# A transformer layer with routed experts on one core: three tiles of the last sum on TensorE, and the first and last loads in halves

## What is computed

```python
probs = softmax((gelu(xf @ wg1 + bg1) @ wg2 + bg2)[:, :20])
top_vals, top_idx = top_k(probs, 2)
gates = zeros((N, E)).at[arange(N)[:, None], top_idx].set(top_vals)
y = sum over e of gates[:, e, None] * (xf @ We[e] + be[e])
x = x + y
```

## Time and profile before

| what | us |
|---|---|
| median of three runs (674.92 to 677.53) | 677.24 |
| the profiled execution | 675.09 |
| its span, first to last instruction | 673.2 |
| last product of the last block ends | 649.05 |
| first load of `ys` issued | 653.20 |
| first scaled add begins | 658.12 |
| last scaled add ends | 669.81 |
| last store lands | 672.8 |

### The profile page before, as it was taken

The page is one execution under the profiler, slowest core; times in us unless marked ns, Lnnn a source line. Parts: engine busy times, 40 slices in busy tenths (PEclk is TensorE's granted clock), DMA queues, the critical chain, the costliest instruction groups (busy, mean ns, idle before and its releaser), DMA issues.

```text
span 673.2 us, 16124 instructions
## 1 busy us (share of the span) xinstructions
PE 642.6 (95%) x6390; PEld 526.1 (78%) x6390; DVE 439.9 (65%) x999; ACT 327.2 (49%) x620; POOL 299.4 (44%) x265
## 2 busy tenths in 40 slices
PE   5999999999999999999999999999999999999980
PEld 5778888887888788887888788887778787788850
DVE  4865666666556555757555557454477678999976
ACT  4435453544434444444433426334355654899930
POOL 2215644366344644366344614612126157788520
PEclk9999999999999999999999999999999999999995
DMA  8512566545764456445753562220000497999729
GB/s 331 210 50 47 137 168 150 128 113 137 174 137 122 121 147 148 111 125 144 174 127 77 136 168 83 80 64 2 2 18 34 146 363 272 382 389 354 285 86 339
DMA packets 41817, 105.68 MB, mean 157 GB/s; under 512 B 8052, under 2 KB 8436, under 8 KB 40962
## 3 DMA queue, kind: packets, MB, share of 16 engines
q1 hardware_dynamic: 37330, 96.12, 48.5%
q0 software_dynamic: 4400, 8.41, 3.4%
HBM read 65.61 MB, written 11.34 MB: 114 GB/s over the span
## 4 chain that ended last, share of the span: by engine, by line
PE 91%; DVE 4%; DMA 2%; ACT 1%; issue 1%; POOL 0%; POOLq 0%; DVEq 0%; SPq 0%; ACTq 0%
PE bank L195 25%; PE bank L197 23%; PE bank L196 23%; PE bank L415 5%; PE bank L397 4%; PE bank L201 3%; DVE x_sb L1854 2%; PE bank L633 1%; PE bank L620 1%; PE bank L649 1%; DMA wr<-scratch_ys 1%; DMA raw<-in_wk 1%; DMA xi<-scratch_xn,row 1%; PE bank L447 1%; DVE stats L1580 0%
## 5 line engine op out<-in xcount | busy, mean ns | idle before, releaser
L1891 POOL TENSOR_SCALAR pp<-pp,rl 128x400 f32<-128x400 f32 x128 | 164.1, 1300 | 182.4 <-DVE rl L1359 182.4
L978 ACT ACTIVATE pp<-pp,acc 128x400 f32<-128x400 f32 x128 | 79.0, 619 | 66.6 <-DVE acc L1418 66.6
L1418 DVE CUSTOM_DVE_ANT_0 pp<-bank,cap 128x400 f32<-128x400 f32 x128 | 65.9, 571 | 50.9 <-PE bank L397 50.9
L195 PE MATMUL bank<-chi,wk 128*128 128x400 f32 x248 | 87.3, 352 | 0.0
L196 PE MATMUL bank<-clo,wk 128*128 128x400 f32 x248 | 85.5, 345 | 0.0
L197 PE MATMUL bank<-chi,wk 128*128 128x400 f32 x248 | 85.5, 345 | 0.0
L1410 DVE STREAM_TRANSPOSE raw<-pp 128x512 f32<-128x512 f32 x128 | 83.4, 688 | 2.2 <-POOL pp L1891 2.2
L195 PE MATMUL bank<-wv,chi 128*128 128x512 f32 x192 | 78.8, 410 | 0.0
L196 PE MATMUL bank<-wv,chi 128*128 128x512 f32 x192 | 75.4, 393 | 0.0
L197 PE MATMUL bank<-wv,clo 128*128 128x512 f32 x192 | 75.2, 392 | 0.0
L195 PE MATMUL bank<-wh,xu 128*128 128x512 f32 x144 | 59.7, 415 | 0.4 <-ACT hT L912 0.2
(11 more groups left out here) (268 smaller groups left out, 1333.6 us busy)
## 6 DMA issues: line engine op xcount, KB each, us to landing
pt<-raw SPq DMA_DIRECT2D x256, 128.0 KB, 2.4
wr<-in_We SPq DMA_DIRECT2D x13, 1024.0 KB, 12.1
craw<-in_ctx SPq DMA_DIRECT2D x15, 800.0 KB, 4.6
raw<-in_We SPq DMA_DIRECT2D x8, 1024.0 KB, 13.2
acc<-in_We SPq DMA_DIRECT2D x6, 1024.0 KB, 12.6
wr<-scratch_ys SPq DMA_DIRECT2D x8, 512.0 KB, 8.1
x_sb<-in_x SPq DMA_DIRECT2D x2, 1024.0 KB, 11.5
scratch_xn<-acc SPq DMA_DIRECT2D x8, 256.0 KB
```

The costliest lines, as they stand in the source:

```text
L195: pe.matmul(o, lhs[0], rhs[0], start=start, stop=False)
L978: act.activation(frame(p8), frame(p8), ACT.Exp, bias=bias, scale=-1.0, accum_out=total).then_inc(S["a_exp"], 1)
L1418: dve.tensor_tensor_reduce(out=frame(p8), in0=scores[:, p8 % 4, :], in1=cap[:, :], scale=-1.0, scalar=nm[:, b, p8:p8 + 1] if seg else 3e38 ...
L1891: pool.tensor_scalar(frame(p8), frame(p8), rl[:, n % 2, p8:p8 + 1], None, ALU.mult).then_inc(S["g_pn"], 1)
```

## The change

Tiles 2, 4 and 6 (`FULL`) no longer get their two scaled adds on VectorE. ScalarE writes two diagonal matrices for each of them, with the tokens' first and second gates on the diagonal. TensorE adds up, in one PSUM bank for each tile (3, 4 and 7), the bias product and the two products of a diagonal matrix and the loaded rows, and VectorE adds the bank to `x_sb`. The other five tiles (`plain`) are treated as before, but each bias product is followed by two spare products into bank 7, and three spare products stand ahead of each full tile's diagonal products. VectorE and the stores take the tiles in the order 0, 1, 3, 2, 5, 4, 7, 6. The loads keep the order 0 to 7; those of tiles 0 and 7 are two transfers, one for each of a token's two rows.

```diff
+        diag = [cs2[:, 128 * j:128 * j + 128] for j in range(4)] + [mbd[:, j, :] for j in range(2)]
+        FULL, ENDING = (2, 4, 6), (0, 1, 3, 2, 5, 4, 7, 6)
+        plain = [i for i in ENDING if i not in FULL]
...
+        by_half = {0: S["d_gate"], 7: S["d_g1"]}
+        half_count = {0: 96, 7: 48}
...
-                def biases(which):
-                    for i in which:
-                        if i >= 3:
-                            pe.wait_ge(S["v_y"], i - 2)
-                        r = slice(32 * (i % 4), 32 * (i % 4) + E)
-                        pe.matmul(pb[i % 3][:, :], gT[r, i // 4, :], be[r, :], start=True, stop=True).then_inc(S["p_be"], 1)
+                def bias(i, bank, stop):
+                    r = slice(32 * (i % 4), 32 * (i % 4) + E)
+                    return pe.matmul(bank[:, :], gT[r, i // 4, :], be[r, :], start=True, stop=stop)
+
+                def spare(n, bank):
+
+                    for _ in range(n):
+                        pe.matmul(bank[:, :], wh[1][0][:, 0, 0:128], wh[1][0][:, 0, :], start=True, stop=True)
+
+                def ending():
+                    for n, i in enumerate(plain):
+                        if n >= 3:
+                            pe.wait_ge(S["v_y"], n - 2)
+                        bias(i, pb[n % 3], True).then_inc(S["p_be"], 1)
+                        spare(2, pb[7])
+                    pe.wait_ge(S["a_gT"], 1 + 2 * len(FULL))
+                    for n, i in enumerate(FULL):
+                        bias(i, pb[(3, 4, 7)[n]], False)
+                    for n, i in enumerate(FULL):
+                        pe.wait_ge(S["v_y"], len(plain))
+                        spare(3, pb[0])
+                        pe.wait_ge(d_ga[i], 16)
+                        for c in range(2):
+                            last = pe.matmul(pb[(3, 4, 7)[n]][:, :], diag[2 * n + c], yga[:, i, c, :], start=False, stop=(c == 1))
+                        last.then_inc(S["p_be"], 1)
...
-                biases(range(8))
+                ending()
...
+            act.wait_ge(S["v_rt"], 8)
+            act.wait_ge(S["v_tok"], 2)
+            for n, i in enumerate(FULL):
+                for c in range(2):
+                    act.activation(diag[2 * n + c], ident, ACT.Copy, scale=gmg[:, c, i:i + 1]).then_inc(S["a_gT"], 1)
...
-            biases(range(8))
-            for i in range(8):
+            biases()
+            for n, i in enumerate(ENDING):
+                if i in FULL:
+                    j = FULL.index(i)
+                    dve.wait_ge(S["p_be"], len(plain) + j + 1)
+                    dve.tensor_tensor(x_sb[:, i, :], x_sb[:, i, :], pb[(3, 4, 7)[j]][:, :], ALU.add).then_inc(S["v_out"], 2)
+                    continue
                 dve.wait_ge(d_ga[i], 16)
                 for c in range(2):
+                    if c and i in by_half:
+                        dve.wait_ge(by_half[i], half_count[i])
                     if c:
-                        dve.wait_ge(S["v_out"], 2 * i + 1)
+                        dve.wait_ge(S["v_out"], 2 * n + 1)
...
             for i in range(8):
-                sp.dma_start(yga[:, i], t["ys"].rearrange("(c i p) n -> i p c n", c=2, i=16)[i]).then_inc(
-                    d_ga[i], 16)
-            for i in range(8):
-                sp.wait_ge(S["v_out"], 2 * i + 2)
+                rows_of = t["ys"].rearrange("(c i p) n -> i p c n", c=2, i=16)[i]
+                if i in by_half:
+                    for c in range(2):
+                        sp.dma_start(yga[:, i, c], rows_of[:, c]).then_inc(by_half[i] if c else d_ga[i], 16)
+                else:
+                    sp.dma_start(yga[:, i], rows_of).then_inc(d_ga[i], 16)
+            for n, i in enumerate(ENDING):
+                sp.wait_ge(S["v_out"], 2 * n + 2)
                 sp.dma_start(out.rearrange("(i b) q d -> i (b q) d", b=2)[i], x_sb[:, i, :]).then_inc(S["d_out"], 16)
```

More of the change, by code:

```diff
@@ L1804, in gates, with biases @@
                                   ALU.mult).then_inc(S["v_rt"], 1)
[L1806 to L1809, removed]
+            def biases():
+                for n, i in enumerate(plain):
+                    dve.wait_ge(S["p_be"], n + 1)
+                    dve.tensor_tensor(x_sb[:, i, :], x_sb[:, i, :], pb[n % 3][:, :], ALU.add).then_inc(S["v_y"], 1)
             def turn_tokens(n):
```

## The result

| | before | changed |
|---|---|---|
| median of 22 runs each, us | 679.07 | 682.83 |
| ratio, 95% interval | | 1.007 (1.0051 to 1.0089) |
| span of the profiled execution, us | 673.2 | 679.4 |
| the ending: last product of the last block to landing of the last store, us | 23.8 | 28.8 |
| of it: until the first load of `ys` is issued | 4.15 | 4.16 |

The account below looks back on a forecast made before the run. The transfers were taken to bound the ending, right behind VectorE. The last store, 0.25 us earlier, was put at -0.15 us on the 677.24 us median: 677.1 us, range 674.8 to 679.3.

Parts of the forecast that it names:

- what bounds the kernel before: In the ending, VectorE's adds and the transfers both bound, VectorE 0.1 to 0.5 us behind the loads, DMA engines full.
- Rival A: Ending: VectorE is the bound, so its reduced work moves the end by 3.2 us, to 674.0 us; chance 0.05.
- The gain of 0.15 us that was forecast: At the end: last store issued 0.25 us earlier, worth 0.15 us, between 0 and 0.4, as transfers keep their end.
- the step on TensorE's new work, its cover: Five biases with spares take 7.8 us from 648.97, done about 657.0, just before tile 0's first half at 657.4.
- the wait for tile 3: VectorE wants tile 3 at 660.8, but it lands about 662.3: a 1.5 us wait absorbing most bias lateness.
- Rival B: TensorE at lower clock for diagonal products: 2.0 to 6.5 us slower; chance 0.25 up to 3.4 us, 0.08 above.
- The last plain bias add by 657.4: VectorE, before the scaled adds: the last plain bias add ends by 657.4, when tile 0's first half is expected.
- VectorE idle 1.5 us ahead of tile 3: VectorE at tile 3's scaled adds: about 1.5 us idle, put down to the load.
- DMA share near 1 until the end: DMA engines in the ending: share near 1 until about 671.6, a sign that the forecast is right.
- A last store after 670: End of the kernel: a last store issued after 670 would show the lower-clock case and the forecast wrong.
- Granted clock in 660 to 669: TensorE during the diagonal products: 1.0 for the forecast, 0.5 for the lower-clock case, with VectorE's adds waiting for them.
- A change ahead of 649 us: Before the ending, where nothing was edited: any change there would show the forecast wrong.

Follow-up runs that it names:

- half the adds: Kernel before, with one scaled add per tile instead of two (second expert's row loaded but not added); ratio 0.9996.
- half the loads: Kernel before, loading only each token's first expert row of `ys`, which both scaled adds read; ratio 0.9951.
- the kernel with the clock kept: Changed kernel with longer spare runs: 8 or 6 behind each plain bias, 14, 4 and 3 ahead of the diagonal products; ratio 1.0003.

## Why the prediction was wrong

Forecast 677.1 us, within 0.5% at 0.88; measured 682.83, a ratio of 1.007. Of the 5.7 us between forecast and measured, 1.8 is the median of the kernel before, which rose from 677.24 to 679.07 with more runs, and 3.8 what the change did (4.8 by the ratio), where 0.15 us of gain was forecast.

*Right: what bounds the kernel before.* That the transfers lie right behind VectorE, and that less work on VectorE brings nothing, was shown by half the adds (0.9996) and half the loads (0.9951), and by the kernel with the clock kept (1.0003). Rival A, VectorE as the bound, would have been 0.995, which lies outside the intervals of the kernel with half the adds and of the one with the clock kept. The gain of 0.15 us that was forecast is too small for any of these runs to show.

*Wrong: the step on TensorE's new work, its cover.* The prediction put what this work costs the rest at nothing: the five plain biases at 7.8 us, the last added at 657.0, and at the lower clock 659.1, most of which the wait for tile 3 would take up. The runs show a loss of 0.7% in its place, 5.0 us in the ending, and the ratio's loss is gone when the spares are out. The last plain bias was in at 662.67 (661.98 + 0.69), 12.5 us after z. Three numbers were off. At the upper level a bias with two spares took 1.71 us, not 1.55. So two were done when the clock fell, not three, and three remained at 3.15 us each (2.00 + 1.15): 9.45 us, where 659.1 allows 5.9 us behind 653.2, the add included. That figure doesn't follow even from the prediction's own terms: at 653.2 some 3.0 us of products were left, which at half the clock are 6.1 us, and with the add of 0.69 us that is 660.0. And the slack against it, a wait of 1.5 us for tile 3, is less than the 5.6 us by which VectorE came late to the first half. The row that told it was there: the earlier trace rows showed the fall to 0.50 while TensorE was still at its biases, and I took the upper level as the likelier one for no reason that a row gave. Even at the upper level the cover was only 0.4 us by the prediction's own numbers (657.0 against 657.4). The lower level should have been the base case of that sum.

*Rival B had the mechanism, and half of the place.* It named the clock, but put its price on the diagonal products alone. There it was met in part: tile 2's took 2.92 us in the chain, with the clock back for the last of its four passes, the other two 1.72 us (the prediction took 2.15 at the upper level and 4.0 at the lower; the first passes have a pitch of 0.85 us, so 3.4 would have been the full price). But tile 2's products started at 668.2 and not at 660.9, since the queue of biases was ahead of them. Without the spares among the biases the clock falls too, and the price of B alone is what the kernels without them show: 0.9988, 1.0015 and 0.9994, nothing that can be told from none. B's chance of 0.08 for over 3.4 us was too low for a case that the clock's fall in the earlier trace rows had made the likely one. B also took the clock's return from the earlier trace rows; the profile gives a granted clock of 1.00 over the whole of that stretch (4.7 to 14 us), so that those rows don't show a return. Here it is seen at 670.7.

*Signs given.* The last plain bias add by 657.4: it was 662.7, the first sign to fail. VectorE idle 1.5 us ahead of tile 3: it wasn't, having come late. DMA share near 1 until the end: 0.40. A last store after 670: 677.0. Granted clock in 660 to 669: 0.50, and VectorE waited 4.31 us for a diagonal product, both of which were named for B. A change ahead of 649 us: the last product ended 1.15 us later, within the 6.5 us by which it scatters among the kernels here. Tile 7 landed 18.9 us after z, in the kernel before 18.7: the loads kept their time, as the prediction said.

## What to carry to other kernels

An engine that is idle is not a free place for work when others wait for the few things that it does there: count what is ahead of the awaited result in its queue, at the slower of its two clock levels, if the trace shows that level anywhere nearby. Filler that is to hold a clock belongs behind the results that others wait for and not between them, and a change in it has to be judged by the granted clock that the trace then shows. And a chain of waits that runs through one engine without a gap doesn't prove that the engine is the bound: compare when each load lands with when it is used, and look at the DMA engines' share, before work is moved away from it.

## What the runs showed of the hardware

TensorE's clock fell after a stretch in which its records leave no gap: 3.40 of 3.40 us busy from 650.20 to 653.60, two biases of 20 rows with two full spare products each, and 0.50 from then on. With six spares for each bias it stayed at 1.00. So the busy share of the records doesn't tell the level. Which part of the stretch made it fall, the products of few rows or pauses that the records don't show, no run separates. The Trainium skill, "TensorE: Matmul & The Clock Gate", section "HAM oscillation — how this bites in real kernels", describes the fall in the waits for DMAs between products; here it fell without any such wait, so that section's case is not the only one.

The trace of the kernel before has no float32 product of 128 rows and 512 columns. In the changed kernel it is two passes with a pitch of 0.43 us at the upper level and 0.85 us at the lower (1.72 us in the chain for a tile's four passes at the upper level). A bias, 20 rows deep and alone between spares, took 1.05 and 2.00 us for its two passes, no less than two passes of 128 rows at their pitch (0.86 and 1.70 us): so few rows don't make a product cheaper. What made the biases of the kernel before cheap is that three of them ran at once, 1.13 us for all three.

Two transfers of 256 KB in the place of one of 512 KB brought the first half 2 us ahead, and in the one execution of that alone the next load 1.1 us later. Whether that is the rule stays open: the time between two landings scatters by as much (2.6 instead of 1.3 us for tile 6 above).
